# Two-layer graph kernel on one core: adjacency and expert products one step earlier, the last pass's loads ahead of the last expert's, and the relu moved into the addition

## The chip, the cores and the metric

The kernel runs on one core of a Trainium2 chip. Its engines work side by side: TensorE (PE) does matrix products and transposes, VectorE (DVE), ScalarE (ACT) and GpSimd (POOL) work row by row on 128 partitions, and SyncE (SP) only issues transfers (DMA). Each engine executes its own program in order and waits on semaphores that the others raise. The metric is the time of one execution on the device in microseconds (us); lower is better.

## The reference, cut to what matters

There are 8 batches of 1024 rows with 512 features, and for each batch a 1024 x 1024 adjacency matrix. The first layer takes four Gaussian weights of each adjacency entry, normalises them over the four, sums each over the row, and scales a 512 x 512 product of x with them. The second picks one of four expert matrices for each batch, multiplies, sums over neighbours, normalises by statistics over all batches that took the same expert, and applies a relu. After each layer the input is added and the row is normalised.

```
w = jnp.exp(-0.5 * diff / (1e-14 + precision_relation ** 2))
w = w / jnp.sum(w, axis=-1, keepdims=True)
ws = jnp.sum(w, axis=2)
weighted = ws[..., None] * neighbourhood_features[:, :, None, :]
out = jnp.einsum('bknd,nod->bkno', weighted, W)
...
scores = x.mean(axis=1) @ router_w + router_b
top1 = jnp.argmax(scores, axis=-1)
support = jnp.einsum('bnh,bhk->bnk', x, expert_w[top1])
out = jnp.einsum('bnm,bmk->bnk', adj, support)
...
y = (out - m) * inv * bn_gamma[top1][:, None, :] + bn_beta[top1][:, None, :]
return jax.nn.relu(y)
...
x = _layernorm(x + _L0_gnn_ref(x, adj, ...), axis=-1)
x = _layernorm(x + _L1_gnn_ref(x, adj, ...), axis=-1)
```

## The kernel before

**The main loop.** The 8 batches are cut into 64 tiles of 128 rows (TILES = 64, T = 8 tiles to a batch). Every engine walks through steps n = 0, 1, 2, ... up to LAST; what tile or unit it touches in a step is written out by hand as n minus a lag. For tile n, ACT squares and exponentiates the adjacency tile (L582, L588, L593), DVE sums the four weights (L888), ACT takes the reciprocal as Ln and Exp (L597, L599), and in the next step DVE forms the row sums (L850) and scales and adds the product h (L872). POOL splits adjacency and x into two half-precision parts (L457 to L473), SP has the DMA engines transpose them, and every second step POOL normalises a pair of rows into x1 and splits it too (L490 to L499, function norm_pair). PE's product h(n) takes 12 matmuls (L1034).

**The second layer rides along.** A batch has 8 units. z(u) (L1049, 24 matmuls) multiplies x1 with the transposed adjacency; it belongs to PE's step n = u + Z_LAG. ACT copies it out of PSUM (L625), DVE forms the low part (L819, function low_z). o(u) (L1065, 12 matmuls) multiplies with the chosen expert in w_sel and belongs to step n = u + O_LAG; ACT copies it (L641), DVE takes its statistics (L839). PE's order in a step is h, z, o. z of a batch's first unit needs x1 of all eight tiles; four units of z must be there before the o that uses them. ps_z has two banks, ps_o one; near the end odd units of o use a bank of ps_t as second bank (second_bank). The routing of a batch needs the mean of its x1, which PE takes in two halves (L1025, function mean): the second half stands in front of z(8b). w_sel is a single buffer, so SP may load the expert of the next batch only after the last o of the batch before.

**The flush.** After tile 63 there is no more h. PE works off what the lags have left: from z(53) and o(49) on.

**What is kept.** Units of o below KEPT go to DRAM (out_spill); the later ones stay in SBUF buffers of the last pass (o_chunk). x1 goes to DRAM and comes back as well.

**The last pass.** When all of o is there, DVE and ACT derive scale and shift for each feature and batch (b_sb, L956). Then, for the batches in the order of n = 0 to 7 (batch_of: 7, 6, 0, 1, ... 5), ACT applies relu(scale * o + shift) (L677, function relu), PE transposes back into one of four PSUM banks (L1108), DVE adds x1 (L989 for even rows, L991 with a row sum for odd ones) and takes statistics (L967, L975), ACT takes squares of odd rows (L686) and the inverse deviation (L706, L709), POOL normalises (L551), and SP stores. SP's list of loads for this pass (fetch_o, fetch_x1) begins behind its whole main loop, thus behind the load of the last expert into w_sel.

Of the kernel before, what the change touches and what calls it, by code (L numbers as in the profile page):

```python
# [12 lines left out]
P = 128  # L13
# [25 lines left out]
Z_LAG = 10  # L39
O_LAG = 14  # L40
# [8 lines left out]
def gnn_program(nc, x, adj, mean_rel, prec_rel, w0, router_w, router_b, expert_w, gamma, beta, x1_spill,  # L49
# [11 lines left out]
    KEPT = TILES - O_LAG - 1  # L61
    assert T == 8 and C == 4 and NK == 4 and HALF == 512 and KW == P and E == 4

    with ExitStack() as ctx:
# [182 lines left out]

        def std_group(n, half):
# [24 lines left out]
        def _(sp):  # L273
# [41 lines left out]
            sp.dma_start(two_var[:], prec_rel.rearrange("(o k) -> o k", o=1).broadcast_to([P, NK])).then_inc(gauss_landed, 16)  # L315
            load_adj(0)
            load_x(0)
            sp.dma_start(w0_in, w0.rearrange("n o d -> o n d")).then_inc(w0_landed, 16)
            load_adj(1)
            load_x(1)  # L320
            load_x(2)
            load_expert(0)
            turn_adj(0)
            turn_x(0)
            sp.dma_start(rw[:], router_w.rearrange("(c p) e -> p c e", p=P)).then_inc(router_landed, 16)
            sp.dma_start(rb[:], router_b.rearrange("(o e) -> o e", o=1)).then_inc(router_landed, 16)
            turn_x(1)

            for n in range(LAST):
                b, u = n // T, n - O_LAG  # L330
                if n % 2 == 0 and 0 <= n - 4 < TILES - T:
                    pair = (n - 4) // 2
                    sp.wait_ge(pool_x1, 2 * pair + 2)
                    at = 2 * pair % X_RING
                    sp.dma_start(x1_pairs[pair], x_in[:, at:at + 2, :]).then_inc(x1_stored[pair % 5], 16)
                if n + 2 < TILES:
                    load_adj(n + 2)
                if n + 3 < TILES:
                    load_x(n + 3)
                if u % T == 0 and 0 <= u < TILES:  # L340
# [3 lines left out]
                    if u == 0:  # L344
                        sp.wait_ge(planes_stored, 16 * E)
# [792 lines left out]
```

## Time and profile before

| | us |
|---|---|
| median of 3 runs (899.32 to 901.04) | 899.39 |
| the profiled execution | 897.02 |
| its span, first to last instruction | 895.2 |
| TensorE's mean granted clock, share of full speed | 0.933 |

| engine | busy us | share of the span |
|---|---|---|
| TensorE (PE) | 756.1 | 84% |
| VectorE (DVE) | 754.8 | 84% |
| ScalarE (ACT) | 780.3 | 87% |
| GpSimd (POOL) | 674.9 | 75% |

The shares are means over three stages that have different limits: the main loop up to about 721 us, the flush up to 809 us, the last pass from 814 us on. Each has to be read by itself. A TensorE clock of 1.0 is the 2.4 GHz level, 0.5 the 1.2 GHz level, and what lies between is a mixture over the stretch.

### The profile page before, as it was taken

The numbers are of one execution on the slowest core, as the hardware profiler recorded it, in microseconds if no ns is written. First come the engines' busy times: TensorE is split into PE (matmuls) and PEld (weight loads), VectorE is DVE, ScalarE is ACT, GpSimd is POOL, SyncE is SP. The second block draws the span as 40 slices with busy tenths as digits, with TensorE's granted clock in tenths as the row PEclk, the third lists the DMA queues.
The fourth block names the chain that finished last, engine by engine and source line by source line (L and its number), as shares of the span: only waits on it lengthen the run. The fifth ranks groups of instructions, "written<-read, shape, count | busy, mean of one in ns | idle before, by whom it ended". The sixth has DMA issues, their size and how long they took to land.

```text
span 895.2 us, 12481 instructions
## 1 busy us (share of the span) xinstructions
PE 756.1 (84%) x3922; PEld 358.0 (40%) x3922; DVE 754.8 (84%) x1635; ACT 780.3 (87%) x790; POOL 674.9 (75%) x761
## 2 busy tenths in 40 slices
PE   1444468899999999999999999999999999996472
PEld 1111123344444444444444444444444444444462
DVE  1999988899999999999999999999999952326995
ACT  5999998999999999999999999999999921117995
POOL 6699999999998888888888888888888420000675
PEclk9766669999999999999999999999999999997976
DMA  7799887987888879878877797879776300699999
GB/s 228 205 271 258 187 236 173 225 195 197 210 239 200 190 197 241 192 190 197 237 194 189 194 235 189 189 188 236 190 187 153 94 1 1 229 383 337 330 378 375
DMA packets 262693, 191.18 MB, mean 214 GB/s; under 512 B 210018, under 2 KB 210274, under 8 KB 261090
## 3 DMA queue, kind: packets, MB, share of 16 engines
q1 hardware_dynamic: 262482, 190.38, 77.9%
q8 instruction: 31, 0.51, 0.2%
q14 instruction: 36, 0.29, 0.1%
q10 hardware_dynamic: 144, 0.00, 0.0%
HBM read 91.52 MB, written 48.50 MB: 156 GB/s over the span
## 4 chain that ended last, share of the span: by engine, by line
ACT 40%; DVE 31%; POOL 13%; PE 10%; issue 4%; DMA 1%; DVEq 0%; ACTq 0%; SPq 0%; POOLq 0%
DVE ps_t L888 21%; ACT wgt L588 13%; ACT ps_t L597 6%; ACT ps_t L599 6%; ACT ps_t L593 5%; ACT adj_in L582 5%; PE ps_z L1049 5%; DVE x_in L872 4%; DVE wgt L850 4%; POOL adj_cut L462 3%; PE ps_o L1065 2%; PE ps_t L1065 2%; POOL adj_in L457 2%; POOL x_turn L473 2%; POOL x1p L499 1%
## 5 line engine op out<-in xcount | busy, mean ns | idle before, releaser
L1049 PE MATMUL ps_z<-adjT,x1p 128*128 128x512 f16 x1536 | 343.7, 381 | 0.0
L1034 PE MATMUL ps_h<-w0T,x_turn 128*128 128x512 f16 x768 | 197.2, 412 | 79.3 <-DVE x_in L872 68.1
L888 DVE TENSOR_TENSOR ps_t<-ps_t,wgt 128x1024 f32<-128x1024 f32 x192 | 234.9, 1223 | 27.8 <-ACT ps_t L593 26.9
L850 DVE SCALAR_TENSOR_TENSOR wgt<-wgt,ps_t 128x1024 f32<-128x1024 f32 x192 | 224.7, 1214 | 16.1 <-ACT ps_t L599 16.0
L1049 PEld LDWEIGHTS ps_z<-adjT,x1p 128*128 128x128 f16 x1536 | 149.7, 98 | 180.5 <-issue 2.4
L582 ACT ACTIVATE wgt<-adj_in,neg_mu 128x1024 f32<-128x1024 f32 x192 | 205.6, 1134 | 8.3 <-POOL adj_in L457 8.2
L588 ACT ACTIVATE wgt<-wgt 128x3072 f32<-128x3072 f32 x64 | 176.5, 2758 | 0.0
L1065 PE MATMUL ps_o<-zT,w_sel 128*128 128x512 f16 x684 | 157.0, 379 | 0.8 <-DMA w_sel<-w_planes 0.8
L1034 PEld LDWEIGHTS ps_h<-w0T,x_turn 128*128 128x128 f16 x768 | 75.8, 104 | 192.7 <-issue 113.8
L462 POOL TENSOR_TENSOR adj_cut<-adj_in,adj_cut 128x1024 f16<-128x1024 f32 x64 | 136.6, 2134 | 5.4
L1065 PEld LDWEIGHTS ps_o<-zT,w_sel 128*128 128x128 f16 x684 | 66.7, 98 | 82.1 <-DMA w_sel<-w_planes 1.8
L872 DVE SCALAR_TENSOR_TENSOR x_in<-ps_h,wsum,x_in 128x128 f32<-128x128 f32 x256 | 82.4, 343 | 9.2 <-PE ps_h L1034 0.5
L499 POOL TENSOR_TENSOR x1p<-x_in,x1p 128x512 f16<-128x512 f32 x64 | 76.0, 1188 | 5.3
L625 ACT ACTIVATE zT<-ps_z 128x512 f16<-128x512 f32 x64 | 37.0, 578 | 49.4 <-PE ps_z L1049 49.4
L473 POOL TENSOR_TENSOR x_turn<-x_in,x_turn 128x512 f16<-128x512 f32 x64 | 74.2, 1160 | 5.3
L457 POOL TENSOR_SCALAR adj_in<-adj_in 128x1024 f32<-128x1024 f32 x64 | 69.5, 1086 | 11.4 <-DMA adj_in<-in_adj_dram 6.0
L819 DVE SCALAR_TENSOR_TENSOR zT<-ps_z,zT 128x512 f16<-128x512 f32 x64 | 43.1, 674 | 39.1 <-ACT zT L625 39.1
L582 ACT ACTIVATE adj_in<-adj_in,neg_mu 128x1024 f32<-128x1024 f32 x64 | 72.8, 1138 | 0.0
L460 POOL TENSOR_SCALAR adj_cut<-adj_in 128x1024 f16<-128x1024 f32 x64 | 67.6, 1057 | 5.3
L597 ACT ACTIVATE ps_t<-ps_t 128x1024 f32<-128x1024 f32 x64 | 64.6, 1009 | 6.3 <-DVE ps_t L888 4.2
L536 POOL TENSOR_SCALAR adj_in<-adj_in 128x4 f32<-128x4 f32 (+1 forms) x9 | 1.8, 196 | 90.0 <-DVE adj_in L975 90.0
L593 ACT ACTIVATE ps_t<-adj_in 128x1024 f32<-128x1024 f32 x64 | 65.8, 1028 | 3.1 <-DVE wgt L850 0.6
(218 smaller groups left out, 857.6 us busy)
## 6 DMA issues: line engine op xcount, KB each, us to landing
adj_in<-in_adj_dram SPq DMA_DIRECT2D x64, 512.0 KB, 4.0
x_in<-in_x_dram SPq DMA_DIRECT2D x64, 256.0 KB, 4.3
x_spill<-x_in SPq DMA_DIRECT2D x28, 512.0 KB, 3.3
out_spill<-o_stage SPq DMA_DIRECT2D x49, 256.0 KB, 3.0
w_sel<-w_planes SPq DMA_DIRECT2D x8, 1024.0 KB, 5.2
adjT<-x_spill SPq DMA_DIRECT2D x6, 1024.0 KB, 12.3
out_dram<-adjT SPq DMA_DIRECT2D x5, 1024.0 KB, 6.1
adjT<-out_spill SPq DMA_DIRECT2D x4, 1024.0 KB, 12.6
```

Of the source, the lines that this page charges most:

```text
L462: g.tensor_tensor(cut[:, 1, :], tile, cut[:, 0, :], ALU.subtract).then_inc(pool_al, 1)
L473: g.tensor_tensor(cut[:, 1, :], tile, cut[:, 0, :], ALU.subtract).then_inc(pool_xl, 1)
L582: s.activation(to, adj_in[:, n % ADJ_RING, :], ACT.Square, bias=neg_mu[:, k:k + 1], scale=spread[k]).then_inc(act_sq, 1)
L588: s.activation(w, w, ACT.Exp, scale=-1.0).then_inc(act_w, 1)
L593: s.activation(tot, adj_in[:, n % ADJ_RING, :], ACT.Exp, scale=-1.0).then_inc(act_solo, 1)
L597: s.activation(tot, tot, ACT.Ln, scale=SUM_SCALE).then_inc(act_ln, 1)
L850: v.scalar_tensor_tensor(out=wgt[:, m % 2, j, :], in0=wgt[:, m % 2, j, :], scalar=SUM_SCALE / W0_SCALE, in1=tot, op0=ALU.mult, op1=ALU.mul ...
L872: last = v.scalar_tensor_tensor(out=row[:, f], in0=ps_h[:, m % 2, f], scalar=wsum[:, m % 2, COLUMN[k]:COLUMN[k] + 1], in1=row[:, f], op0=A ...
L888: v.tensor_tensor(tot, tot, wgt[:, n % 2, j, :], ALU.add).then_inc(dve_tot, 1)
L1034: last = te.matmul(ps_h[:, n % 2, :], xT[:, n % 2, left, c, :], w0T[:, right, c, :], start=(c + i == 0), stop=(c == C - 1 and i == 2))
L1049: last = te.matmul(ps_z[:, u % 2, :], x1p[:, b % 2, left, t, k * P:(k + 1) * P], adjT[:, b % 2, right, t, half * HALF:(half + 1) * HALF], ...
L1065: last = te.matmul(ps_out(u), w_sel[:, left, c, k * P:(k + 1) * P], zT[:, right, half, c, :], start=(c + i == 0), stop=(c == C - 1 and i = ...
```

## The change

The lags go from 10 and 14 to 9 and 13. To make that possible PE's order in a step becomes h, o, z (z ahead of o only where o begins a batch and at step 64); the first batch starts with an empty step 9, one z in step 10 and two in step 11; z(8b) waits for x1 tile by tile, and the second half of the mean stands behind it. In the flush, o(52) to o(55) stand together in step 65, ahead of z(56). SP's loads for passes 1, 2 and the o of 3 are issued ahead of the last expert's. In the last pass scale and shift are applied without relu: in pass 0 by DVE (columns 0 to 255), ACT (256 to 511) and POOL (512 to 1023), in passes 2 and 5 by POOL alone, in the others by ACT; DVE's addition takes the maximum with zero on its way. The stores of the expert planes stand earlier in their steps, and the o of passes 6 and 7 is fetched in halves.

```
-Z_LAG = 10
-O_LAG = 14
+Z_LAG = 9
+O_LAG = 13
...
+        BY_POOL = (2, 5)
+        DVE_COLS, ACT_COLS, POOL_COLS = slice(0, 2 * P), slice(2 * P, HALF), slice(HALF, NR)
...
-            return u > KEPT and u % 2 == 1
+            return u > KEPT + 2 and u % 2 == 1
+        FLUSH = TILES - T + Z_LAG
+        def z_unit(n):
+            if n <= Z_LAG + 2:
+                return ((), (0,), (1, 2))[n - Z_LAG] if n >= Z_LAG else ()
+            return range(n - Z_LAG, min(TILES, n - Z_LAG + 1))
+        def o_units(n):
+            u = n - O_LAG
+            if n == FLUSH:
+                return range(u, TILES - T)
+            if FLUSH < n < TILES - T + O_LAG:
+                return range(0)
+            return range(max(0, u), min(TILES, u + 1))
+        def z_ahead_of_o(n):
+            return n == FLUSH - 1 or (n - O_LAG) % T == 0
...
+                    if m == NB - 1:
+                        for i in range(1, 3):
+                            fetch_o(i)
+                            fetch_x1(i)
+                        fetch_o(3)
                     sp.wait_ge(dve_route, m + 1)
                     wait(sp, pe_o, u)
...
+            pool.wait_ge(act_o, TILES)
+            pool.wait_ge(dve_affine, C)
+            affine(0, POOL_COLS)
+            pool.wait_ge(dve_bn, BN_ALL)
+            pool.wait_ge(*landed_o(BY_POOL[0]))
+            affine(BY_POOL[0], slice(0, NR))
             for n in range(NB):
+                if n == 2:
+                    pool.wait_ge(*landed_o(BY_POOL[1]))
+                    affine(BY_POOL[1], slice(0, NR))
...
+            dve.wait_ge(act_o, TILES - G)
+            for k in range(C):
+                v.tensor_scalar(o_chunk(0, k)[:, DVE_COLS], o_chunk(0, k)[:, DVE_COLS], b_sb[:, NB - 1, k:k + 1],
+                                b_sb[:, NB - 1, C + k:C + k + 1], ALU.mult, ALU.add).then_inc(dve_affine, 1)
             batch_shares(0, NB - 1)
...
-                        v.tensor_tensor(row, ps_y[t % 4], row, ALU.add).then_inc(dve_y2, 1)
+                        v.scalar_tensor_tensor(out=row, in0=ps_y[t % 4], scalar=0.0, in1=row, op0=ALU.max,
+                                               op1=ALU.add).then_inc(dve_y2, 1)
...
             def z_product(u):
-                if u % T == 0:
-                    pe.wait_ge(pool_1l, u + T)
-                    mean(b, 1).then_inc(pe_mean, 1)
+                if k == 0:
                     for j in range(2):
-                        pe.wait_ge(adj_turned[j], 16 * (u + T) // 2)
+                        pe.wait_ge(adj_turned[j], 16 * (u + G) // 2)
                 for t in range(T):
+                    if u % T == 0:
+                        pe.wait_ge(pool_1l, u + t + 1)
...
-                wait(pe, act_o, u - 1 if u > KEPT + 1 else u)
+                wait(pe, act_o, u - 1 if u > KEPT + 3 else u)
...
-                    if t == 0:
-                        pe.wait_ge(act_relu, C if n == 0 else C * n + 3 * C)
+                    if n == 0 and t == 0:
+                        pe.wait_ge(dve_affine, C)
+                    if n == 0 and t == 2:
+                        pe.wait_ge(act_affine, C)
                     if n == 0 and t == G:
-                        pe.wait_ge(act_relu, 3 * C)
+                        pe.wait_ge(pool_affine, C)
+                    if n > 0 and t == 0:
+                        pe.wait_ge(*affine_done(n))
```

How the instructions of PE move at the start of the second layer, steps 10 to 12 (ps_h is h, ps_z is z, ps_s the means and the router's score). Before:

```order
L1025 MATMUL ps_s<-ones_h,x1p 128x1 x32
L1049 MATMUL ps_z<-adjT,x1p 128x512 x24
L1034 MATMUL ps_h<-w0T,x_turn 128x512 x12
L1049 MATMUL ps_z<-adjT,x1p 128x512 x24
L1075 MATMUL ps_s<-rw,sumT 1x4 x4
```

After:

```order
L1118 MATMUL ps_z<-adjT,x1p 128x512 x24
L1095 MATMUL ps_s<-ones_h,x1p 128x1 x32
L1104 MATMUL ps_h<-w0T,x_turn 128x512 x12
L1118 MATMUL ps_z<-adjT,x1p 128x512 x48
L1146 MATMUL ps_s<-rw,sumT 1x4 x4
```

z(0) now stands ahead of the mean, and z(1) and z(2) follow each other in step 11.

The same engine where the flush begins, from h(63) on (ps_o and ps_t are the two banks of o). Before:

```order
L1034 MATMUL ps_h<-w0T,x_turn 128x512 x12
L1049 MATMUL ps_z<-adjT,x1p 128x512 x24
L1065 MATMUL ps_o<-zT,w_sel 128x512 x12
L1049 MATMUL ps_z<-adjT,x1p 128x512 x24
L1065 MATMUL ps_o<-zT,w_sel 128x512 x12
L1049 MATMUL ps_z<-adjT,x1p 128x512 x24
L1065 MATMUL ps_t<-zT,w_sel 128x512 x12
L1025 MATMUL ps_s<-ones_h,x1p 128x1 x32
```

After:

```order
L1104 MATMUL ps_h<-w0T,x_turn 128x512 x12
L1136 MATMUL ps_o<-zT,w_sel 128x512 x12
L1118 MATMUL ps_z<-adjT,x1p 128x512 x48
L1136 MATMUL ps_o<-zT,w_sel 128x512 x24
L1136 MATMUL ps_t<-zT,w_sel 128x512 x12
L1136 MATMUL ps_o<-zT,w_sel 128x512 x12
L1136 MATMUL ps_t<-zT,w_sel 128x512 x12
```

Behind h(63) there are now o(50), z(54), z(55), and then five o in a row, o(51) to o(55), before z(56).

SP behind the last store of o, where the last expert's load stands between the loads for the last pass. Before:

```order
L354 DMA out_spill<-o_stage 128x512 x2
L346 TENSOR_LOAD sc_int
L346 ISA x2
L347 ISA
L347 DMA w_sel<-w_planes 128x4096
L376 DMA wgt<-out_spill 128x256 x2
L430 DMA adjT<-x_spill 128x4x512 x2
```

After:

```order
L464 DMA out_spill<-o_stage 128x512 x2
L359 DMA wgt<-out_spill 128x512 x2
L414 DMA adjT<-x_spill 128x4x512 x2
L379 DMA x_turn<-out_spill 128x2x1024
L379 DMA w0T<-out_spill 128x2x1024
L414 DMA x1p<-x_spill 128x4x512 x2
L379 DMA adjT<-out_spill 128x2x1024 x2
L452 TENSOR_LOAD sc_int
L452 ISA x2
L453 ISA
L453 DMA w_sel<-w_planes 128x4096
```

Ten loads stand ahead of the last expert's now.

## Rows read from the trace of the kernel before

**Rows 1.** The page: its first line, with the span.

```profile
span 895.2 us, 12481 instructions
```

**Rows 2.** Windows: length, busy us per engine (instructions), PE clock, DMA share, GB/s.

```profile
400.00:600.00 200.00, 195.33 (x1030) 88.51 (x1029) 189.95 (x400) 197.84 (x183) 175.84 (x192) 1.00 0.82 203
...
740.00:760.00 20.00, 20.00 (x101) 9.05 (x100) 5.02 (x14) 3.58 (x6) 0.00 (x0) 1.00 0.00 1
...
816.60:885.40 68.80, 41.43 (x252) 37.50 (x252) 62.84 (x196) 66.03 (x126) 43.30 (x73) 0.82 0.96 350
...
860.00:880.00 20.00, 14.60 (x90) 13.35 (x88) 19.12 (x61) 18.83 (x39) 16.36 (x28) 0.80 1.05 396
```

**Rows 3.** Timeline of PE, one step: start us, duration us, work [idle before, releaser].

```profile
465.46 2.75 PE L1034 MATMUL ps_h<-w0T,x_turn 128*128 128x512 f16 x12 [0.44 <-DVE x_in L872]
468.05 5.34 PE L1049 MATMUL ps_z<-adjT,x1p 128*128 128x512 f16 x24
473.23 2.75 PE L1065 MATMUL ps_o<-zT,w_sel 128*128 128x512 f16 x12
476.42 2.75 PE L1034 MATMUL ps_h<-w0T,x_turn 128*128 128x512 f16 x12 [0.44 <-DVE x_in L872]
```

**Rows 4.** Timelines of ACT and DVE at the end of that step.

```profile
476.83 0.58 ACT L641 ACTIVATE o_stage<-ps_o 128x512 f32<-128x512 f32 x1
...
477.92 0.67 DVE L819 SCALAR_TENSOR_TENSOR zT<-ps_z,zT 128x512 f16<-128x512 f32 x1
```

**Rows 5.** Timeline of POOL in that step: x1 of the batch's last tile.

```profile
473.69 1.16 POOL L499 TENSOR_TENSOR x1p<-x_in,x1p 128x512 f16<-128x512 f32 x1
```

**Rows 6.** Timeline of PE where the second layer begins.

```profile
123.11 4.74 PE L1034 MATMUL ps_h<-w0T,x_turn 128*128 128x512 f16 x12 [5.86 <-DVE x_in L872]
129.04 0.95 PE L1025 MATMUL ps_s<-ones_h,x1p 128*128 128x1 f16 x32 [1.18 <-POOL x1p L499]
129.85 7.03 PE L1049 MATMUL ps_z<-adjT,x1p 128*128 128x512 f16 x24
```

**Rows 7.** Timeline of ACT there: the copy of z(0), and a later Ln.

```profile
136.92 0.60 ACT L625 ACTIVATE zT<-ps_z 128x512 f16<-128x512 f32 x1 [2.82 <-PE ps_z L1049]
...
148.38 1.01 ACT L597 ACTIVATE ps_t<-ps_t 128x1024 f32<-128x1024 f32 x1 [0.52 <-DVE ps_t L888]
```

**Rows 8.** Timeline of PE in the flush: its two waits and its end.

```profile
734.17 0.95 PE L1025 MATMUL ps_s<-ones_h,x1p 128*128 128x1 f16 x32 [1.26 <-POOL x1p L499]
...
773.03 2.76 PE L1065 MATMUL ps_o<-zT,w_sel 128*128 128x512 f16 x12 [0.81 <-DMA w_sel<-w_planes]
...
806.71 2.75 PE L1065 MATMUL ps_t<-zT,w_sel 128*128 128x512 f16 x12
```

**Rows 9.** Timelines of ACT and DVE in the flush: one z copied and split.

```profile
730.35 0.60 ACT L625 ACTIVATE zT<-ps_z 128x512 f16<-128x512 f32 x1 [4.58 <-PE ps_z L1049]
...
730.98 0.69 DVE L819 SCALAR_TENSOR_TENSOR zT<-ps_z,zT 128x512 f16<-128x512 f32 x1 [3.11 <-ACT zT L625]
```

**Rows 10.** Timeline of DVE: scale and shift of pass 0 are ready.

```profile
813.48 0.19 DVE L956 TENSOR_REDUCE b_sb<-o_stage 128x8 f32<-128x32 f32 x1
```

**Rows 11.** Timeline of PE: the first transposes of the last pass.

```profile
815.41 1.12 PE L1108 MATMUL ps_t<-ident,wgt 128*128 128x128 f32 x4 [5.95 <-ACT wgt L677]
```

**Rows 12.** Groups of ACT in the last pass: count | busy us, mean ns | idle before.

```profile
L677 ACT ACTIVATE wgt<-wgt,b_sb 128x1024 f32<-128x1024 f32 x8 | 9.4, 1227 | 0.0
...
L677 ACT ACTIVATE wgt<-wgt,b_sb 128x384 f32<-128x384 f32 x4 | 2.5, 692 | 0.0
```

**Rows 13.** Groups of POOL with one input, over the whole span.

```profile
L457 POOL TENSOR_SCALAR adj_in<-adj_in 128x1024 f32<-128x1024 f32 x64 | 69.5, 1086 | 11.4 <-DMA adj_in<-in_adj_dram 6.0
...
L551 POOL TENSOR_SCALAR adjT<-adjT,adj_in 128x512 f32<-128x512 f32 x20 | 15.3, 781 | 7.3 <-ACT adj_in L709 7.3
```

**Rows 14.** One line of DVE: duration ns shortest/median/longest, first and last start.

```profile
L1003 DVE TENSOR_SCALAR adjT<-adjT,adj_in x2: 534/724/914, 886.6 to 887.0; 128x512 f32<-128x512 f32 x2
```

**Rows 15.** Timeline of SP: the last store issued.

```profile
888.71 1.12 SPq L404 DMA_DIRECT2D out_dram<-adjT  x1
```

More of the change, by code:

```diff
@@ L430, in fetch_x1 @@
                     sp.dma_start(y_buf[n][g], src).then_inc(x1_back[i], 16)
-            for n in range(RING):
+            sp.dma_start(two_var[:], prec_rel.rearrange("(o k) -> o k", o=1).broadcast_to([P, NK])).then_inc(gauss_landed, 16)
+            load_adj(0)
+            load_x(0)
+            sp.dma_start(w0_in, w0.rearrange("n o d -> o n d")).then_inc(w0_landed, 16)
+            load_adj(1)
+            load_x(1)
+            load_x(2)
+            load_expert(0)
+            turn_adj(0)
@@ L433, in _ @@
+            fetch_x1(3)
+            for n in range(4, RING):
                 fetch_o(n)
-                if n > 0:
-                    fetch_x1(n)
+                fetch_x1(n)
             fetch_o(6)
@@ L667, in relu @@
                     act.wait_ge(dve_bn, BN_ALL)
-                if chunks[0] == 0:
-                    wait(act, act_o, TILES if n < 2 else 0)
-                    wait(act, *landed(o_back, n))
-                pieces = [slice(0, NR)]
-                if n == 0:
-                    chunks = range(C) if chunks[0] == 0 else ()
-                    pieces = [slice(0, P), slice(P, HALF), slice(HALF, NR)]
-                for piece in pieces:
-                    for k in chunks:
-                        s.activation(o_chunk(i, k)[:, piece], o_chunk(i, k)[:, piece], ACT.Relu,
-                                     bias=b_sb[:, b, C + k:C + k + 1], scale=b_sb[:, b, k:k + 1]).then_inc(act_relu, 1)
+                if n < 2:
+                    act.wait_ge(act_o, TILES)
+                if n > 0:
+                    act.wait_ge(*landed_o(n))
+                columns = ACT_COLS if n == 0 else slice(0, NR)
+                for k in chunks:
+                    s.activation(o_chunk(i, k)[:, columns], o_chunk(i, k)[:, columns], ACT.Identity,
+                                 bias=b_sb[:, b, C + k:C + k + 1], scale=b_sb[:, b, k:k + 1]).then_inc(act_affine, 1)
             def odd_squares(n, h):
@@ L709, in inverse_std @@
                 s.activation(r_std[:, at, first:last], r_lnv[:, at, first:last], ACT.Exp, scale=-0.5).then_inc(act_std, 1)
-            for n in range(NB + 1):
-                if n < NB:
-                    relu(n, (0, 1))
-                if 0 <= n - 2:
-                    odd_squares(n - 2, 1)
-                    inverse_std(n - 2, G if n == 2 else 0, T)
-                if n < NB:
-                    relu(n, (2, 3))
+            affine(0, range(C))
+            affine(1, range(C))
+            odd_squares(0, 0)
+            inverse_std(0, 0, G)
+            for n in range(2, NB + 1):
+                ahead = n + 1 < NB and n + 1 not in BY_POOL
+                if ahead:
+                    affine(n + 1, (0, 1))
+                odd_squares(n - 2, 1)
+                inverse_std(n - 2, G if n == 2 else 0, T)
+                if ahead:
+                    affine(n + 1, (2, 3))
                 if n == NB:
@@ L721, in _ @@
                     norm(NB - 2, range(G, T))
[L722 to L725 removed]
+                odd_squares(n - 1, 0)
+            inverse_std(NB - 1, 0, G)
             inverse_std(NB - 1, G, T)
@@ L1052, in z_product @@
                 last.then_inc(pe_z, 1)
+                if u % T == 0:
+                    mean(b, 1).then_inc(pe_mean, 1)
             def o_product(u):
```

215 lines of the change are left out of this document (112 added, 103 removed).

## Prediction

> **What bounds the kernel now.** I read the windows first, then the timeline of each engine in one step, then the places where PE waits. There are three stages. In the main loop ACT is busy for 197.84 of 200 us and PE for 195.33 at clock 1.00 [rows 2]. One step lasts 10.96 us (476.42 - 465.46 [rows 3]). What closes the ring of a step is ACT and DVE in turn: Ln waits for DVE's sum where no o is copied, by 0.52 us [rows 7]; the copies of z and o fill that gap. In the flush PE alone is the bound: 20.00 of 20 us busy, ACT 3.58, DVE 5.02, and the DMA engines are idle, share 0.00 [rows 2]. In the last pass ACT works for 66.03 of 68.80 us, DVE for 62.84, POOL for 43.30 [rows 2]: ACT is the bound, DVE stands close behind it, and the transfers are close too, 350 GB/s on average and 396 in a full window [rows 2].
>
> **Start of the second layer.** z(0) now follows h(10) directly. h(10) ends at 127.85 (123.11 + 4.74), and only z's last two tiles need the x1 for which the mean waited until 129.04 [rows 6]; tile 6 comes after 18 of 24 matmuls, 3.9 us into z. So z(0) ends between 133.2 (at the 5.34 of [rows 3]) and 134.9 (at its 7.03 of [rows 6], part of them at the low level since PE had stood still). ACT is ready for it at 134.10 (136.92 - 2.82 [rows 7]): its wait of 2.82 us shrinks to 0 to 0.8. Against that, step 11 has two z. h(11) is released one step after h(10), at 134.07, and takes 2.59 to the start of what follows (468.05 - 465.46), each z 5.18 (473.23 - 468.05 [rows 3]): z(2) ends at 147.0, ACT copies it in 0.57 and starts Ln at 147.7 where the trace has 148.38 [rows 7]. Gain 0.7 us. If ACT's new wait were hidden it would be 2.3; if PE fell to its low level for half of the two z, the step would end 5 us later, a loss of 4.3. PE works without a gap from 123.11 on, and after such work its rows are at the high level, so I take -0.7. The first o, in step 13, has its expert's load behind 13 us of h, z and other work; I cost it at nothing.
>
> **Main loop.** No copy is added or dropped in a normal step, only their order. By [rows 3] z would end where o does now, at 475.8 (473.23 + 2.59). Its copy takes the second slot, 476.83 to 477.41, and low_z reads it at 477.92 [rows 4]: 1.0 us of slack ahead of ACT, 0.5 ahead of DVE. The tightest step is this one, where z(8b) starts at 470.65 already and needs the last tile's x1 for its last three matmuls, at 475.2; POOL has it at 474.85 (473.69 + 1.16 [rows 5]). The mean's second half moves behind z and costs the 0.8 that it cost one step later. I take 0 for each step; the bounds are 0 and 0.3 (half of what is left where the slacks meet, 50 times over: 15 us, which is the rival below). SP's wait for the last o before each expert load ends 5 us earlier in its step, since o now stands second; the transfers behind it gain, and nobody waited for them.
>
> **Flush.** One z and one o fewer are left: 5.18 + 2.59 = 7.77. Two waits go: 1.26 for x1 of tile 63, now covered by o(52) to o(55), 10.4 us long, and 0.81 for the last expert [rows 8]; its load has z(59) and z(60) as cover now, and the ten loads ahead of it (8.9 MB, 23 us at the 396 GB/s of [rows 2]) run from about 724 to 747, some 10 us before the router has chosen. Three waits come. The hand-over from a z to the o that needs it takes 1.38 (ACT starts at 730.35, DVE ends at 731.67 [rows 9], 0.06 for the two hops): o(60) now follows z(63) directly. o(52) and o(53) each wait for the copy of the o ahead, 0.60 + 0.1 = 0.7 each. Net: 7.77 + 2.07 - 2.78 = 7.06. From 809.5 (806.71 + 2.75 [rows 8]) PE ends at 802.4, with the start at 801.7. Scale and shift come 4.2 us behind PE's end as now (813.67 [rows 10] - 809.46): call that moment S. Before S = 813.7; after 813.7 - 7.1 - 0.7 = 805.9.
>
> **Last pass.** Before, PE's first transposes start 1.7 us after S and DVE first works at 816.66; from 816.60 to 885.40 it is idle for 5.96 (68.80 - 62.84 [rows 2]), always for ACT's scaling. The change takes from ACT 2 passes of 4 x 1.13 (9.1 us) and most of pass 0. The maximum rides in an instruction whose odd-row form DVE runs already: 0. DVE gets 4 pieces of 256 columns; a 512-column one takes 0.53 undisturbed and 0.91 against POOL [rows 14], so 0.3 each, 1.2 in all, bounds 0.9 and 2.4; 1.1 of transposes follow [rows 11], and the first addition begins at S + 2.6, beside ACT's 4 pieces (at most 4 x 0.69 [rows 12]) and POOL's four of 512 columns, 4 x 0.78 [rows 13], which end at S + 4.4 ahead of row 4 at S + 5. Then DVE needs 62.8 without a gap: S + 65.4. Who is next? ACT's work is 66.0 - 9.1 - about 4 = 53, under DVE's. POOL's grows: 43.3 + 3.1 + 8 pieces of 1024 columns. Such a piece with immediates takes 1.09, a 512 one with scalars 0.78 [rows 13]; so it lies between 1.1 and 1.56, I take 1.3 (nearer the row of its own length): 10.4, in all 57. Its second block of four stands ahead of the normalisation of pass 2, which ends at about S + 40; the row buffers that this frees are needed at S + 48. So POOL is covered by 5 to 8 us.
>
> The Trainium skill, GPSIMD Engine Reference, section 3.1, counts about 1.8 cycles an element at 1.2 GHz for a good loop on this engine; for 512 elements that is 0.768 us and the trace agrees (0.767 as the usual value). By that rule a piece of 1024 would be an estimate of 1.54 us, POOL would have 59 us, and the end of its last block would come some 0.7 us later.
>
> After DVE's end the trace has 9.8 us (895.2 - 885.40 [rows 1]), the last of them from the issue of the last store at 888.7 to 889.8 [rows 15] on: S + 75.2. The transfers come on top. From S + 37 on seven blocks of 2.1 MB have to go through (x1 of pass 7 and the stores of passes 2 to 7), 14.7 MB; at 396 GB/s [rows 2] that is 37 us plus about 2 for the last landing: S + 76. I add 0.7, bounds 0 and 3. So the span ends at S + 75.9 = 881.8, where before it ended at S + 81.5: 5.6 gained.
>
> **Sum.** 0.7 + 7.1 + 5.6 = 13.4. Span 881.8; the profiled execution 897.02 - 13.4 = 883.6; the median of the runs stood 2.37 above the profiled one, so 899.39 - 13.4 = 886.0.
>
> **Rivals.**
> (1) The transfers bound the last pass. For: 396 GB/s in the full window, and all stores come closer together; against: 8.9 MB of loads start some 45 us earlier, in the idle flush. At 350 GB/s [rows 2] the 14.7 MB take 42 us and the end is at S + 81, so up to 5 us of the gain go: 889 to 891. The Trainium skill, SBUF — State Buffer, section "Who interferes with whom", has compute and DMA never contend; by it only this rate can do it.
> (2) The start does not gain: PE falls to its low level in the two z. 13.4 - 0.7 - 4.3 = 8.4 gained: 891.
> (3) The loads or waits in the flush cost more than thought, for example the ten loads land later and the last expert behind them: up to 8 us, 890 to 894. Against: the queue is empty for 20 us there.
> (4) Slower: ACT and DVE's hand-over of z in a normal step. If the z copy reached DVE late by x, each of some 50 steps would grow by x; the gain is gone at x = 0.27. For it z would have to end 1.5 + 0.27 us later than [rows 3] lets it; PE has only 0.44 us of idle in a step. x = 0.35 gives 903.
> (5) The change does not do what it says in the last pass: POOL's pieces hold PE back, for example with 2 us a piece under DVE's load. Then pass 2 starts at S + 21 instead of S + 18 and pass 5 at S + 43, DVE loses 3 to 4: 889 to 890.
>
> **How the numbers follow.** Forecast 0.62, 884.0 to 888.5; rival 1 0.13, rival 5 0.06, rival 2 0.05, rival 3 0.05, rival 4 0.04, and 0.05 for a time below 884, if both new waits and the transfers cost nothing (13.4 + 0.7 + 1.4 + 0.7 gained: 883.2). The range 883.5 to 890.5 takes in the forecast, most of rivals 1 and 5 and part of that last one, and leaves out about 0.17. A measurement of this kernel tells 0.2% (1.8 us) from no change. Faster by more than that: all but rival 4, less 0.02 for rivals 2 and 3 both at their worst, which would come out within it; so 0.94, 0.02 and, for rival 4, 0.04.
>
> **What would show it.** ACT's wait for z(0) under 1 us and a wait of 1 to 2 us for z(2); a step of 10.96 us from 200 to 700; PE's last o at about 801.7 with waits of 0.7, 0.7 and 1.4 and none for w_sel; S at 806; DVE idle under 1 us between its first addition and its last, and busy above 0.97 there; ACT below 0.85 of it; last store landed at 882. The forecast is wrong if the step is longer than 11.0, if DVE waits for PE or for x1 in passes 2 to 7, or if more than 12 us lie between DVE's last statistics and the end.

## The result and the profile after

The changed kernel takes 891.33 us (median; 888.44 to 893.22), the kernel before 899.39 beside it. The ratio is 0.9908, 95% interval 0.9891 to 0.9925: 8.1 us are gained where 13.4 were forecast, and the time lies 0.8 us above the range. The direction was right. Three steps of the working were not: the first expert's load was costed at nothing, the wait of o(52) at 0.7 us, and the transfers at the end at 0.7 us.

The profiled execution of the changed kernel took 888.44 us. Its page begins with the span; the windows have the columns of [rows 2].

```profile
span 886.7 us, 12501 instructions
```

```profile
400.00:600.00 200.00, 195.06 (x1028) 88.56 (x1027) 189.92 (x400) 197.66 (x184) 175.72 (x191) 1.00 0.82 202
...
760.00:780.00 20.00, 20.00 (x94) 9.12 (x93) 5.72 (x25) 3.22 (x6) 0.00 (x0) 1.00 0.27 104
811.30:872.90 61.60, 41.20 (x253) 28.50 (x251) 61.28 (x192) 53.52 (x111) 53.81 (x82) 0.94 1.03 377
...
840.00:860.00 20.00, 13.67 (x85) 8.82 (x85) 20.00 (x66) 17.36 (x39) 19.69 (x32) 1.00 1.04 376
```

The main loop is as it was. In the last pass (from DVE's first addition to its last) DVE now works for 61.28 of 61.60 us, ACT for 53.52 and not for 66 of 69, and the DMA share is 1.03 where [rows 2] has 0.96: two things are full now, DVE and the transfers.

PE's timeline, at the first o, in one step of the main loop, and at the three waits of the flush and its end:

```profile
166.86 2.76 PE L1136 MATMUL ps_o<-zT,w_sel 128*128 128x512 f16 x12 [1.33 <-DMA w_sel<-w_planes]
...
465.93 2.75 PE L1104 MATMUL ps_h<-w0T,x_turn 128*128 128x512 f16 x12 [0.44 <-DVE x_in L937]
468.51 2.75 PE L1136 MATMUL ps_o<-zT,w_sel 128*128 128x512 f16 x12
471.10 5.34 PE L1118 MATMUL ps_z<-adjT,x1p 128*128 128x512 f16 x24
...
727.68 2.76 PE L1136 MATMUL ps_o<-zT,w_sel 128*128 128x512 f16 x12 [2.11 <-DVE zT L884]
731.22 2.75 PE L1136 MATMUL ps_t<-zT,w_sel 128*128 128x512 f16 x12 [0.78 <-ACT wgt L685]
...
793.99 2.76 PE L1136 MATMUL ps_o<-zT,w_sel 128*128 128x512 f16 x12 [1.42 <-DVE zT L884]
...
801.77 2.75 PE L1136 MATMUL ps_t<-zT,w_sel 128*128 128x512 f16 x12
```

ACT's timeline where the second layer starts: z(0) is copied without a wait, z(2) with one, Ln of step 11 comes at 147.63 ([rows 7]: 148.38). Two steps further, in step 13, Ln comes at 170.63.

```profile
133.92 0.57 ACT L668 ACTIVATE zT<-ps_z 128x512 f16<-128x512 f32 x1
...
147.14 0.60 ACT L668 ACTIVATE zT<-ps_z 128x512 f16<-128x512 f32 x1 [1.68 <-PE ps_z L1118]
147.63 1.02 ACT L656 ACTIVATE ps_t<-ps_t 128x1024 f32<-128x1024 f32 x1
...
170.63 1.03 ACT L656 ACTIVATE ps_t<-ps_t 128x1024 f32<-128x1024 f32 x1
```

DVE's timeline: scale and shift, the four pieces, the first addition, the last statistics; and SP's, the first expert's load and the last store:

```profile
808.54 0.19 DVE L1021 TENSOR_REDUCE b_sb<-o_stage 128x8 f32<-128x32 f32 x1
808.76 1.38 DVE L1027 TENSOR_SCALAR wgt<-wgt,b_sb 128x256 f32<-128x256 f32 x4
...
811.45 0.69 DVE L1058 SCALAR_TENSOR_TENSOR x_in<-ps_t,x_in 128x512 f32<-128x512 f32 x1 [0.43 <-PE ps_t L1185]
...
873.54 0.18 DVE L1044 BATCH_NORM_AGGREGATE adj_in<-y_stat 128x2 f32<-128x6 f32 x1
```

```profile
160.49 0.40 SPq L453 DMA_DIRECT2D w_sel<-w_planes  x1
...
878.25 1.29 SPq L388 DMA_DIRECT2D out_dram<-adjT  x1
```

So S, the moment at which scale and shift are ready, is 808.7 (808.54 + 0.19); before it was 813.7 [rows 10]: 4.9 us gained ahead of it. From S to the end it is 78.0 us (886.7 - 808.7) where it was 81.5: 3.5 gained behind it. The forecast had 7.8 and 5.6.

### The profile page after: what moved, and what is told of

Read it like the earlier page. It is cut to its first block, busy times and chain, and to the rows that moved or that the text cites. A ratio compares the mean times of both kernels' runs of the same rounds, so it can differ in the third digit from the quotient of the medians.

```text
span 886.7 us, 12501 instructions
## 1 busy us (share of the span) xinstructions
PE 751.8 (85%) x3922; PEld 349.1 (39%) x3922; DVE 754.0 (85%) x1639; ACT 766.9 (86%) x774; POOL 687.5 (78%) x773
## 4 chain that ended last, share of the span: by engine, by line
ACT 38%; DVE 27%; POOL 19%; PE 9%; issue 4%; DMA 1%; SPq 0%; POOLq 0%; DVEq 0%; ACTq 0%
DVE ps_t L953 19%; ACT wgt L647 13%; ACT ps_t L656 6%; ACT ps_t L658 6%; ACT adj_in L641 5%; ACT ps_t L652 5%; PE ps_z L1118 5%; POOL adj_cut L505 3%; DVE x_in L937 3%; DVE wgt L915 3%; PE ps_o L1136 2%; POOL adj_in L500 2%; POOL x_turn L516 2%; PE ps_t L1136 2%; POOL adj_cut L503 2%
## 5 line engine op out<-in xcount | busy, mean ns | idle before, releaser
L1104 PE MATMUL ps_h<-w0T,x_turn 128*128 128x512 f16 x768 | 194.5, 407 | 75.1 <-DVE x_in L937 64.2
L1136 PE MATMUL ps_o<-zT,w_sel 128*128 128x512 f16 x696 | 159.7, 379 | 4.8 <-DVE zT L884 3.5
L656 ACT ACTIVATE ps_t<-ps_t 128x1024 f32<-128x1024 f32 x64 | 64.6, 1009 | 5.9 <-DVE ps_t L953 3.8
L658 ACT ACTIVATE ps_t<-ps_t 128x1024 f32<-128x1024 f32 x64 | 64.5, 1008 | 2.0
```

The lines of the kernel that those rows point to most:

```text
L656: s.activation(tot, tot, ACT.Ln, scale=SUM_SCALE).then_inc(act_ln, 1)
L658: s.activation(tot, tot, ACT.Exp, scale=-1.0).then_inc(act_rec, 1)
L1104: last = te.matmul(ps_h[:, n % 2, :], xT[:, n % 2, left, c, :], w0T[:, right, c, :], start=(c + i == 0), stop=(c == C - 1 and i == 2))
L1136: last = te.matmul(ps_out(u), w_sel[:, left, c, k * P:(k + 1) * P], zT[:, right, half, c, :], start=(c + i == 0), stop=(c == C - 1 and i = ...
```

## Experiments

Time and ratio of each run, the ratio to the kernel before on the same chip; S and what lies behind it are read from each profiled execution as above. The first four runs share a chip, the next four another, flush3, all4 and all5_whole a third, and all4_norm has a fourth; across chips the ratios compare better than the medians.

| run | median us (lowest to highest) | ratio, 95% | S | S to end |
|---|---|---|---|---|
| after_again | 890.46 (888.53 to 895.51) | 0.9907, 0.9881 to 0.9934 | 811.2 | 78.0 |
| relu_back | 895.11 (892.86 to 898.74) | 0.9956, 0.9939 to 0.9972 | 813.6 | 82.0 |
| half_stores | 889.16 (886.16 to 892.58) | 0.9894, 0.9870 to 0.9918 | 809.3 | 75.1 |
| fetch_late | 891.03 (889.27 to 894.14) | 0.9903, 0.9885 to 0.9922 | 814.2 | 78.2 |
| wsel0 | 890.40 (888.54 to 891.44) | 0.9903, 0.9885 to 0.9920 | 812.4 | 77.3 |
| lowz | 888.44 (887.45 to 892.09) | 0.9897, 0.9877 to 0.9917 | 807.8 | 78.2 |
| halves | 892.30 (889.03 to 897.39) | 0.9922, 0.9904 to 0.9940 | 816.7 | 78.9 |
| all5 | 884.54 (884.29 to 885.39) | 0.9848, 0.9832 to 0.9864 | 804.4 | 78.4 |
| flush3 | 885.17 (884.44 to 885.78) | 0.9841, 0.9825 to 0.9858 | 805.6 | 78.4 |
| all4 | 885.27 (884.22 to 886.88) | 0.9846, 0.9828 to 0.9864 | 804.7 | 78.5 |
| all5_whole | 885.06 (883.72 to 885.84) | 0.9838, 0.9821 to 0.9855 | 806.4 | 77.7 |
| all4_norm | 885.07 (883.87 to 885.30) | 0.9826, 0.9807 to 0.9846 | 804.9 | 77.2 |

### The same kernel again

> The changed kernel once more, as the base for the other three. Expected: 888 to 893 us, ratio about 0.991, first o at 166.9, o(52) at 727.7, scale and shift ready at 808.7, DVE's last statistics at 873.7, end of the span 886.7 or later.

S came at 811.2 and not at 808.7, although nothing was changed. Two rows of PE hold it: h(12) runs at the low clock (0.7 us later at Ln of step 13), and o(52) waits as before and then runs at the low clock as well:

```profile
157.52 4.12 PE L1104 MATMUL ps_h<-w0T,x_turn 128*128 128x512 f16 x12 [2.35 <-DVE x_in L937]
...
728.46 4.45 PE L1136 MATMUL ps_o<-zT,w_sel 128*128 128x512 f16 x12 [2.11 <-DVE zT L884]
```

4.45 against 2.76 is 1.7 us. The window of that o(52) has a granted clock of 0.61; from 727.0 to 728.4, in the wait ahead of it, the clock was 1.00:

```profile
728.50:732.90 4.40, 4.40 (x12) 1.48 (x12) 0.58 (x2) 0.00 (x0) 3.88 (x7) 0.61 1.05 410
```

A stall of PE can thus cost more than its own length, and differs from one execution to the next. Of the seven profiled kernels that have this wait of 2.1, four ran o(52) in 4.06 to 4.45 (after_again, fetch_late, wsel0, halves), three in 2.76. In the six kernels without this wait o(52) ran in 2.75 or 2.76.

### The last pass of before

```diff
-            pool.wait_ge(act_o, TILES)
-            pool.wait_ge(dve_affine, C)
-            affine(0, POOL_COLS)
...
-            affine(0, range(C))
-            affine(1, range(C))
...
+                    relu(n, (0, 1))
```

> The flush, the lags and the early loads stay as changed; the last pass is the old one: ACT alone scales, shifts and takes the maximum, DVE only adds, POOL has no affine pieces. Theory A (start and flush are worth what the trace says, 813.7 - 808.7 = 5.0 us, and the last pass takes its old 81.5 us from there): span 890.2, that is 5 us under the kernel before, and 3.5 us above the changed kernel. Theory B (the loads that start early give part of the gain in the last pass whoever scales): the span ends well before 890, near 887 to 888. Theory C (the last pass is bound by transfers in either form, so that the new division of the scaling is worth nothing): the same time as the changed kernel, 886.7 to 889.

S to the end is 82.0 us, 4.0 more than with the new division, and the median is 4.7 above after_again. Theory A holds (81.5 was expected); B and C fall. ACT is the bound again, at the same 66 us of [rows 2]:

```profile
816.54:885.04 68.50, 40.18 (x252) 36.13 (x252) 62.79 (x196) 65.98 (x125) 43.15 (x73) 0.85 0.97 355
```

S itself was 813.6 here, nearly 5 us later than in the first profile of the changed kernel, with the same program ahead of it. Ln of one step followed Ln of the step before by 16.49 us at one place, the first o:

```profile
170.32 4.03 PE L1117 MATMUL ps_o<-zT,w_sel 128*128 128x512 f16 x12 [2.86 <-DMA w_sel<-w_planes]
```

### Half of the stores

```diff
-                    sp.dma_start(dst, y_buf[n][g]).then_inc(...)
+                    rows = slice(0, G // 2 if n < NB - 2 else G)
+                    sp.dma_start(dst[:, rows], y_buf[n][g][:, rows]).then_inc(...)
```

> Of each group of four rows of y only two are stored, in passes 0 to 5: 6.3 MB less to write, 16 us of transfers at 400 GB/s, with no engine's work changed; half of these rows is left out of the output. Theory A (the end is bound by transfers: the queue is full from 800 us on, and the last stores wait behind it): DVE's last statistics still at 65.0 us behind the moment S at which scale and shift are ready, but the span ends at S + 75.2 or a little less, some 2 to 3 us earlier than the changed kernel; the last store lands 5.4 us or less after its issue instead of 7.2. Rival B (the 3 us come from ACT's and POOL's last normalisations, the stores land when they are issued): the end stays at S + 78.

From the first addition to the last statistics DVE takes 62.3 us (811.98 to 874.24), as in the changed kernel (811.45 to 873.72). The last store, one row of SP, lands 5.4 us behind its issue (884.4 - 879.0) and not 7.2 (886.7 - 879.5), and S to the end is 75.1 instead of 78.0. Of these 2.9 us the faster landing is 1.8; the other 1.1 is the issue itself, which ends 69.7 us behind S and not 70.8:

```profile
874.06 0.18 DVE L1045 BATCH_NORM_AGGREGATE adj_in<-y_stat 128x2 f32<-128x6 f32 x1
```

```profile
877.95 1.04 SPq L388 DMA_DIRECT2D out_dram<-adjT  x1
```

Theory A holds, the rival falls: the 2.9 us at the end are transfers that queue. The median fell by 1.3 only, inside the spread of these kernels; the verdict rests on the profile. In the Trainium skill, SBUF — State Buffer, section "Who interferes with whom", compute and DMA never contend; the trace agrees, since DVE's 62.3 us don't change when 6.3 MB of transfers beside it go.

### The loads behind the main loop again

```diff
-                    if m == NB - 1:
-                        for i in range(1, 3):
-                            fetch_o(i)
-                            fetch_x1(i)
-                        fetch_o(3)
...
-            for n in range(4, RING):
+            for n in range(1, RING):
```

> The loads of the last pass stand behind the main loop again, behind the last expert's load, which is issued at 758.6; the rest is the changed kernel. Theory A (the DMA engines are idle from 748 to 792 in the changed kernel, so the 8.9 MB find room there as well, and are through by about 783): no difference, within 0.5 us. Rival B (the early start is what takes the backlog away from the last pass): the span ends 2 us later or more, and the full stretch of the DMA engines reaches further.

The windows show the transfers in another place (the changed kernel has share 0.63 and 235 GB/s in the first of these windows, 0.29 and 108 in the second), and S to the end is 78.2 as before:

```profile
724.00:760.00 36.00, 33.11 (x176) 14.85 (x175) 12.37 (x34) 6.02 (x10) 6.15 (x9) 0.95 0.00 1
760.00:800.00 40.00, 38.59 (x186) 17.31 (x185) 10.41 (x37) 5.86 (x10) 0.00 (x0) 1.00 0.76 278
```

Theory A holds: the early loads are worth nothing by themselves, either place is idle time of the DMA engines. The medians differ by 0.6 us, which is inside the spread.

### The first expert's load a step earlier

```diff
+                if u == -1:
+                    sp.wait_ge(dve_route, 1)
+                    sp.wait_ge(planes_stored, 16 * E)
+                    e = sp.value_load(sc_int[0:1, 0:1], min_val=0, max_val=E - 1)
+                    sp.dma_start(w_sel[:], w_planes[e]).then_inc(w_landed, 16)
                 if n + 2 < TILES:
                     turn_x(n + 2)
```

> One edit in SP's list: the first expert's load stands in step 12, between the turn of adj tile 13 and the turn of x tile 14, and not in step 13 behind the loads of adj tile 15 and x tile 16. Theory A (o(0) waits for this load, 0.45 us in one profiled execution of the changed kernel's program and 1.33 to 3.85 in others, and this wait reaches the end): the load is issued at about 157.2, o(0) starts at 165.5 to 166 without a wait for w_sel, Ln of step 13 comes at 169.6 to 170.3, scale and shift at 807.7 at best, and the median falls by 1 to 4 us against the changed kernel, its spread too. Rival B (ACT has to wait for something else then, as the x turn or PE's next h): o(0) is early, but Ln of step 13 stays at 170.6 and the time too.

```profile
165.25 2.75 PE L1139 MATMUL ps_o<-zT,w_sel 128*128 128x512 f16 x12
...
213.04 0.82 PE L1121 MATMUL ps_z<-adjT,x1p 128*128 128x512 f16 x3 [1.84 <-POOL x1p L545]
...
214.50 4.44 PE L1107 MATMUL ps_h<-w0T,x_turn 128*128 128x512 f16 x12
```

o(0) starts 1.6 us earlier and without a wait; Ln of step 13 is at 169.47, 1.2 earlier. The gain is lost soon after: z(8) comes to the x1 of tile 15 before POOL has it, PE waits 1.84 us (0.49 in the changed kernel), and the h behind runs at the low clock. The two steps take 12.03 and 12.85 us. Both theories were wrong in part: the wait goes, and another takes its place four steps later. The median is the same as after_again's. The profile of all5_whole, which has the same early load, shows it again: z(8) waits 1.63 us, the h behind it takes 4.44 and these two steps 11.82 and 12.85.

The changed kernel and all of its variants that load this expert in step 13 took, from Ln of step 12 to Ln of step 13, 12.00 (twice), 12.19, 12.81, 12.85, 16.21, 16.49 and 17.69 us instead of 10.96, and the profile of the result happened to be one of the two cheapest.

Not all of this is the load: h(12) now waits 2.35 us for DVE (1.37 before), and where it then ran in 4.1 to 4.4 us at the low clock this alone made the step 12.1 to 12.2 (all5, all4, all4_norm, without a wait for w_sel); where it ran in 2.75 and nothing waited for w_sel the step took 10.96 (wsel0). Measured from the base that fits its h(12), the load cost nothing in one profile, 0.6 to 1.9 us in four, 4.3 and 5.2 in two (relu_back, fetch_late) and 6.7 in halves, where h(12) was not slow. In the last three part of it is o(0) at the low clock (4.03 to 4.45 us).

SP's rows show two parts: the load was issued between 160.1 and 162.7 and took 6.3 to 8.7 us to land, and the three costly profiles have the latest issues (161.4, 161.7, 162.7) and the longest landings (7.8, 8.6, 8.7). One suspect was not tested by any run. Right behind the load SP issues the turn of an adj tile, and this issue takes 5.1 to 8.1 us here, 1.9 in the kernel before, where it came 3.4 us after the load. In all eight profiles the load lands 0.1 to 0.3 us behind the end of that issue. Whether the turn holds up the load, or something else holds up both, stays open. SP's rows of the changed kernel and of halves:

```profile
161.49 5.08 SPq L338 DMA_TRANSPOSE adjT<-adj_cut  x1
```

```profile
163.09 8.14 SPq L338 DMA_TRANSPOSE adjT<-adj_cut  x1
```

### low_z(55) ahead of the weighted sum

```diff
                     row_sums(n - 1)
+                    if n == FLUSH - 1:
+                        low_z(TILES - T - 1)
```

> One edit in DVE's list: low_z(55) stands behind the row sums of tile 63, ahead of its weighted sum and statistics. Theory A: o(52) waits for this plane alone beyond the copy of o(51); the plane is ready at 725.4 instead of 727.6, the wait of o(52) shrinks from 2.11 us to 0.7 (the copy of o(51)), all behind it comes 1.4 us earlier, the wait of 1.42 at o(60) and of 0.78 at o(53) stay, and the median is 1.4 us lower at most. Rival B (z(56) then waits for the x1 of tile 63, which comes 0.6 us later): the 1.4 us appear again as a wait ahead of z(56) at 738.

```profile
726.73 2.75 PE L1138 MATMUL ps_o<-zT,w_sel 128*128 128x512 f16 x12 [0.78 <-ACT adj_cut L685]
```

Theory A holds: the wait is 0.78 instead of 2.11 (0.7 expected). From the start of h(63) to S it is 100.1 us (807.8 - 707.7), in the changed kernel 101.4 (808.7 - 707.3): 1.3 gained. z(56) doesn't wait.

### The adj planes by halves

```diff
-        adjT = sb("adjT", [P, 2, 2, T, NR], F16)
+        adjT = sb("adjT", [P, 2, 2, 2, T, HALF], F16)
...
                     elif n == 4:
-                        sp.wait_ge(pe_z, TILES)
+                        sp.wait_ge(pe_z, TILES - G)
```

> The turned adj planes are stored half by half (columns 0 to 511 of all tiles, then 512 to 1023), so that the buffer of pass 4's o is free when z(59) is done and not when z(63) is; its 2.1 MB are loaded from about 773 us on, where the DMA engines are idle, and not at 793. Nothing else is changed. Theory A (from 794 us on the end is bound by transfers, 34 MB of them): 5.2 us of transfers less stand behind 794, the windows from 820 to 860 show a share under 1, the last store lands in 5.4 to 6 us instead of 7.2, and the span ends at S + 75 to S + 76 instead of S + 78. Rival B (only the last three stores crowd each other): S + 78 as before. Rival C (the turns of adj write with another stride and are slower): the step grows above 10.96 us.

```profile
171.41 4.36 PE L1137 MATMUL ps_o<-zT,w_sel 128*128 128x512 f16 x12 [5.42 <-DMA w_sel<-w_planes]
```

The windows of the last pass:

```profile
800.00:820.00 20.00, 12.90 (x60) 6.49 (x59) 9.23 (x29) 6.54 (x12) 1.67 (x3) 0.91 0.76 274
...
840.00:860.00 20.00, 13.66 (x86) 8.80 (x85) 20.00 (x65) 18.87 (x41) 19.79 (x28) 1.00 1.04 381
860.00:880.00 20.00, 11.47 (x72) 7.33 (x70) 20.00 (x62) 13.23 (x31) 18.89 (x33) 0.95 1.04 387
```

My theory A fell, and so did C (steps of 10.96 us). S is at 816.7 here. In the 20 us ahead of S the DMA engines have more idle time than in the changed kernel (share 0.60, there 0.74), but from 840 on they are as full as ever, and S to the end is 78.9. So what binds is not the 34 MB from 794 on. It is rather what can only move behind S: the stores, which half_stores tested, and the reads of passes 6 and 7, whose buffers come free there and which no run tested alone. In the changed kernel 29.0 MB move in the 78.0 us behind S. The profiled execution (897.39) is the slowest of the six, and the stall of 5.42 us at o(0) is in it; its median of 892.30 can't be told from the changed kernel's by its spread.

### Five edits at once, and less

all5 holds lowz, wsel0 and halves and these two:

```diff
-            return u > KEPT + 2 and u % 2 == 1
+            return u > KEPT + 1 and u % 2 == 0
...
-            return n == FLUSH - 1 or (n - O_LAG) % T == 0
+            return n in (FLUSH - 1, LAST_Z) or (n - O_LAG) % T == 0
```

> The three edits of the other runs together, and two more in the flush: o(52) goes to the second bank of PSUM, which is free once the row sums of tile 63 are done, so that o(52) and o(53) no longer wait for the copy of the o ahead (0.7 and 0.78 us), and z(63) stands ahead of o(59), which covers the hand-over of its planes that o(60) waits for (1.42). Expected by the sum: start 1.0 or more, flush 2.1 + 0.8 + 1.4 = 4.3, transfers 2 to 3, so S at 803.4 and the end of the span at 878.5 to 880, the median 8 us under the changed kernel's. If the last pass is bound by transfers after all, the end is at 881 to 882 with S at 803.4; if z(63) ahead of o(59) only moves the wait to o(59), S is at 804.8.

> The changed kernel with the three edits of the flush alone: low_z(55) ahead, o(52) in the second bank, z(63) ahead of o(59). The first expert's load and the buffers are as changed. Expected: the stretch from h(63) to the end of the last o takes 92.7 us, as in the run with all five edits, and not 97.1; no wait of PE over 0.3 us in it, and so no o(52) at the low clock; scale and shift 4.4 us earlier for the same Ln of step 13. If the spread of the changed kernel comes from o(0)'s wait for its expert alone, this kernel keeps it (some 884 to 889); if it comes from the flush (o(52) at the low clock, 1.7 us), it is gone here.

> All five edits less the split of the adj planes by halves: pass 4's o is loaded behind z(63) again. Theory A (what bounds the end are the 25 MB that are written and read behind S, the loads before it are hidden either way): the same time as with all five, 884.5, the end at S + 78. Theory B (the earlier load of pass 4's o is worth something once S is early): 1 us or more slower than 884.5.

From the start of h(63) to S all5 takes 96.9 us (804.4 - 707.5), flush3 96.9 (805.6 - 708.7), the changed kernel 101.4: the flush gives 4.5, expected were 4.3 to 4.4. PE's timeline of flush3 from o(51) to o(53): 0.13 us are left ahead of o(52), nothing ahead of o(53); o(60) stands right behind o(59) in the same way.

```profile
724.24 2.75 PE L1139 MATMUL ps_o<-zT,w_sel 128*128 128x512 f16 x12
727.12 2.76 PE L1139 MATMUL ps_t<-zT,w_sel 128*128 128x512 f16 x12
729.72 2.75 PE L1139 MATMUL ps_o<-zT,w_sel 128*128 128x512 f16 x12
```

The gain of 2 to 3 from the transfers did not come: 78.4 behind S. S itself is at 804.4 where 803.4 was expected (h(12) ran at the low clock in this profile, 4.44 us), and the median is 5.9 us under after_again's, not 8. In all5 28.5 MB move behind S, 0.5 less than in the changed kernel. all4 has the same time as all5, flush3 too: neither the halves nor the early expert add anything that can be told. Of the two readings of the spread in flush3's expectation the second is borne out: its times lie within 1.3 us (the changed kernel's within 7.1), though its o(0) still waits 2.17 us in the profile. With five times in the one and eleven in the other that is likely rather than settled.

### The o of passes 6 and 7 in two pieces

```diff
-                        for at in range(0, NR, HALF):
-                            sp.wait_ge(pe_back, (n - RING) * T + at // P + G)
+                        sp.wait_ge(pe_back, (n - RING + 1) * T)
```

> All five edits, and the o of passes 6 and 7 are loaded as before the change: in two pieces of 1 MB with rows of 4 KB, when the pass before has left the buffer, instead of four pieces of 0.5 MB with rows of 2 KB, the first of them after half that pass. Theory A (the rate falls to 200 to 300 GB/s for some 4 us beside these loads because of their short rows): that pocket goes, and the end comes up to 2 us earlier, at S + 76. Theory B (the pocket belongs to this buffer or batch, since the kernel before had one at 209 to 217 GB/s as well; and the later start leaves the DMA engines idle ahead of it): S + 78 to S + 80, as fast or slower than 884.5.

885.06 against 884.54, S to the end 77.7 against 78.4: no difference that can be told. The DMA view of this run from 800 to 880 us (busy tenths and GB/s in slices of 2 us) still has the pockets, at 824 to 828 and 836 to 840, with the engines busy; at 814 and 822, where the rate is low too, they are only busy for 0.6 of the slice:

```profile
DMA  0299999699969999999999999999999999999999
GB/s 0 41 371 424 407 383 390 172 414 426 397 245 350 231 400 422 405 406 345 254 378 401 407 399 331 346 372 318 404 403 408 410 409 407 402 409 410 409 409 409
```

So the pockets don't need the short rows. Their cause stays open.

### x1 of tile 15 ahead of the next cut

```diff
+                if n == 2 * T + 1:
+                    norm_pair(T - 1)
                 if n + 2 < TILES:
                     cut_x(n + 2)
```

> The five edits less the split of the adj planes, and one more: in POOL's step 17 the normalisation of tiles 14 and 15 (L526 to L542) stands ahead of the cut of x tile 19, since z(8) waited for x1 of tile 15 by 1.84 us where o(0) came early, and the h behind it ran at the low clock (4.44 us for 2.75). Theory A (this wait is what gives back the gain of the early expert load): no wait for x1p at z(8), every step behind the first o takes 10.96, Ln of step 19 comes 1.8 to 3 us earlier than in the run with the expert's load alone, and the median is 882.5 to 884.5. Rival B (the cut of x tile 19, now up to 6.7 us later, holds up h(19) in its place): a step of 12 us two steps later and the same 885. Where h(12) runs at the low clock, the start is 1.2 us later in either case.

```profile
208.16 5.34 PE L1126 MATMUL ps_z<-adjT,x1p 128*128 128x512 f16 x24
213.34 0.94 PE L1103 MATMUL ps_s<-ones_h,x1p 128*128 128x1 f16 x32
214.15 2.75 PE L1112 MATMUL ps_h<-w0T,x_turn 128*128 128x512 f16 x12
```

z(8) doesn't wait, and every step behind step 13 takes 10.96; rival B falls. But in this execution h(12) ran in 4.32 us, so o(0) came late by itself, and the case in which the edit should pay was not in the profile: in all4, without the edit, h(12) ran slow as well, z(8) lost 0.24 us at most and no step grew. Theory A is neither shown nor refuted by the trace, and the time is that of all4. The best kernels here (all5, flush3, all4, all5_whole and this one) are alike, 884.5 to 885.3, 14 to 15.5 us under the kernel before.

## The prediction, point by point

**The bound.** Right: an unchanged main loop, then PE alone, then a pass that moves from ACT to DVE.

**Start.** The mechanism was right (-0.7 expected, Ln of step 11 at 147.63 where 147.7 was expected, z(0) without a wait, z(2) with 1.68). The step that failed is the last sentence of that part: "The first o, in step 13, has its expert's load behind 13 us of h, z and other work; I cost it at nothing." The load is issued at 160.49, behind those of adj tile 15 and x tile 16, 5 us ahead of the first o, not 13. It costs 1.0 in the profile shown and up to 6.7 in others. The work that I had counted as cover stood ahead of the issue.

**Main loop.** Right: the z copy in the second slot costs nothing in a normal step. One step, at about 400 us, takes 11.30 where it took 11.14.

**Flush.** 7.77, 1.26 and 0.81 are confirmed: neither x1 nor w_sel is waited for. So is 1.38 (1.42) and the second 0.7 (0.78). The first 0.7 failed: o(52) waited 2.11. I had named the copy of o(51) and not the other thing that o(52) reads, z(55)'s low plane, which stood in DVE's list behind the row sums and the weighted sum of tile 63; lowz shows both, one behind the other. With 1.0 from the start and 0.2 from the main loop this is 2.6 of the 2.8 by which S was late; 0.2 are spread over small differences.

**Last pass.** S + 2.7 for the first addition (2.6 expected), the four pieces 1.38 (1.2), DVE without a gap, its last statistics at S + 65.0 (65.4), ACT 53.5 (53; 0.87 of the stretch, where I had asked for under 0.85), POOL 53.8 in the window and 54.8 from S to DVE's last statistics (57). POOL's pieces of 1024 columns took 1.19 to 1.20 where I took 1.3:

```profile
L601 POOL TENSOR_SCALAR wgt<-wgt,b_sb x4: 762/764/865, 810.3 to 812.7; 128x512 f32<-128x512 f32 x4
L601 POOL TENSOR_SCALAR x_turn<-x_turn,b_sb x2: 1190/1191/1192, 813.4 to 814.6; 128x1024 f32<-128x1024 f32 x2
```

The rule of the Trainium skill (GPSIMD Engine Reference, section 3.1), which gave an estimate of 1.54 for this piece, is 0.34 us too long here (1.54 against 1.20), though it fits the piece of half the length; the measurement decides. The 0.7 us that I put on the last block by that rule was also a slip: four pieces of 1.54 instead of 1.3 make 1.0. Rival 5 fell with it.

**The end.** The step that failed is the term "I add 0.7" for the transfers: they cost 2.8 (78.0 against the 75.2 without them), and half_stores gives 2.9 back. The end is at S + 78.0 and not at S + 75.9. The blocks behind S + 37 were counted nearly rightly but priced at too good a rate: 15.3 MB moved there, not 14.7, at 373 GB/s over the 41.0 us (376 from 840 to 860) where I took 396, a rate of the best window. Rival 1 was the right mechanism at about half its price. My own sign for it came up: 13.0 us from DVE's last statistics to the end, over 12.

**The sum.** 13.4 forecast, 8.5 between the profiled executions (the missing 4.9: 2.8 ahead of S, 2.1 behind it), 8.1 between the medians. Rival 2 as written (PE at its low level in the two z) did not occur, but its kin did, PE at the low level behind a stall, at h(12) and at o(52). Rival 3 came true in one wait, 1.4 of its up to 8 us; the ten loads did not hold up the last expert. Rival 4 fell.

## What to carry to other kernels

Cover for a load is the time from its issue to its use, not the work that stands beside it in the same step: look at what the issuing queue has ahead of it and right behind it, and take the landing from the stretch where it will stand (6.3 to 8.7 us here, where the same load took 5.1 in the kernel before). For an operation that is moved forward, list everything that it reads and find each producer's place in its own engine's list; here the input that I had not listed was the late one. Where a stretch of transfers is full, count the bytes that cannot start before it, and price them at the mean rate of such a stretch, not at its best window; loads that are only moved within idle time earn nothing.

## What the runs showed of the hardware

- PE's wait costs differed between executions by its clock: 2.76 us or up to 4.45 for the same twelve matmuls behind the same wait of 2.1 us. In the five kernels without the flush's waits the times of five executions lay within 1.1 to 2.7 us; in the eight that kept them (lowz a shorter one) five to twelve lay within 2.9 to 8.4. That the waits make the spread is likely, not shown: four of the five had the early expert load too.
- The same 1 MB load of the first expert, issued at the same place of the list, let o(0) wait between 0.2 and 5.4 us. In the execution with 5.4 all transfers together moved 31 to 84 GB/s from 168 to 171 us, with the DMA engines nearly idle from 169 on; beside the load only the turn of an adj tile was under way. What holds the two up was not found.
- In the last pass the granted clock was 1.00 from 820 to 860, where the kernel before had 0.83 (820 to 840) and 0.86 (840 to 860); PE issued 173 matmuls in these 40 us, before 155.
- The DMA engines of the changed kernel were busy for 0.9 or more from 827 to 835 us and moved only 230 to 335 GB/s, beside the load of pass 7's o and the first stores. With rows of 4 KB instead of 2 (all5_whole) such pockets stayed. The cause wasn't found.
